# An attention block on one core: smaller weight transfers, a rearranged set-up and loop, and no zero products on TensorE

## What is computed

```python
mod = swish(c) @ w_mod + b_mod            # six rows of 144 per image
xn  = ln(x) * (1 + sc_msa) + sh_msa
q, k, v = heads(xn @ w_qkv + b_qkv)       # 16 heads of 9
q, k = ln(q) * g_q, ln(k) * g_k
o   = softmax(q @ k.T / 3) @ v
x   = x + g_msa * (o @ w_proj + b_proj)
x   = x + g_mlp * (gelu((ln(x) * (1 + sc_mlp) + sh_mlp) @ w1 + b1) @ w2 + b2)
```

## Time and profile before

| | us |
|---|---|
| median of three runs (165.75 to 166.16) | 165.94 |
| the profiled execution | 165.81 |
| its span, first to last instruction | 164.0 |
| outside the span | 1.81 |

### The profile page before, as it was taken

One profiled execution on the slowest core, in us unless ns is written; L12 is line 12 of the kernel. 1 busy time (PEld: TensorE's weight loads), 2 busy tenths in 40 slices (PEclk: granted clock), 3 DMA queues, 4 the chain that ended last, 5 costly groups with the idle time before them and its releaser, 6 DMA issues.

```text
span 164.0 us, 3704 instructions
## 1 busy us (share of the span) xinstructions
PE 142.3 (87%) x1364; PEld 70.7 (43%) x1364; DVE 117.8 (72%) x319; ACT 109.5 (67%) x181; POOL 73.6 (45%) x111
## 2 busy tenths in 40 slices
PE   7558972597978998989989989999999979999991
PEld 2251641232332543523525335336456457574771
DVE  5377688129879496895995979948637999965642
ACT  3143132259799889988898899977998592937300
POOL 4064034516549155087580404586787489000000
PEclk9985555569999999999999999999999999999999
DMA  2329203473723105023050070220000000202022
GB/s 51 111 49 309 77 11 66 102 296 136 152 60 91 41 0 128 4 63 68 2 128 4 0 130 4 64 64 4 0 4 2 0 0 4 72 0 72 4 72 74
DMA packets 22139, 10.33 MB, mean 63 GB/s; under 512 B 17548, under 2 KB 21798, under 8 KB 22120
## 3 DMA queue, kind: packets, MB, share of 16 engines
q1 hardware_dynamic: 21842, 9.77, 23.0%
q10 hardware_dynamic: 278, 0.31, 0.6%
HBM read 4.69 MB, written 1.19 MB: 36 GB/s over the span
## 4 chain that ended last, share of the span: by engine, by line
PE 60%; ACT 12%; DVE 6%; issue 4%; DMA 3%; POOL 2%; DVEq 0%; ACTq 0%; SPq 0%
PE ps_o L1305 15%; PE ps_o L1362 10%; PE ps_s L1285 9%; PE ps_s L1343 6%; ACT pT L647 6%; PE ps_o L1314 5%; PE ps_x L1206 2%; PE ps_x L1212 2%; PE ps_x L1208 2%; PE ps_x L1207 2%; ACT z L596 2%; DMA qT<-qst 2%; PE ps_s L1346 1%; ACT zhi L595 1%; DMA out<-yo 1%
## 5 line engine op out<-in xcount | busy, mean ns | idle before, releaser
L647 ACT ACTIVATE pT<-ps_s 128x1024 f32<-128x1024 f32 x64 | 62.3, 1020 | 9.9 <-PE ps_s L1285 7.3
L1305 PE MATMUL ps_o<-pT,v 128*32 128x256 f32 x512 | 37.6, 388 | 0.4 <-DVE xall L992 0.3
L1285 PE MATMUL ps_s<-qT,kT 32*128 32x256 f16 x256 | 24.9, 279 | 9.6 <-ACT pT L647 4.9
L1285 PEld LDWEIGHTS ps_s<-qT,kT 32*128 32x128 f16 x256 | 7.7, 93 | 32.3 <-ACT pT L647 16.6
L438 POOL TENSOR_TENSOR qg<-qn,gbc 128x288 f32<-128x288 f32 x8 | 7.5, 940 | 24.8 <-DVE qn L851 17.7
L1305 PEld LDWEIGHTS ps_o<-pT,v 128*32 128x32 f32 x512 | 11.9, 108 | 14.4 <-issue 8.8
L406 POOL TENSOR_SCALAR z<-xall,mv,rstd 128x144 f32<-128x144 f32 x14 | 14.2, 1022 | 8.0 <-DVE rstd L1436 8.0
L1362 PE MATMUL ps_o<-w_hi,h_hi 128*128 128x144 f16 (+1 forms) x80 | 16.5, 230 | 0.0
L510 POOL TENSOR_SCALAR z<-xall,mv,rstd 128x144 f32<-128x144 f32 x16 | 14.6, 926 | 3.9 <-DVE rstd L1436 3.9
L835 DVE TENSOR_REDUCE ssum<-sq 128x64 f32<-128x576 f32 x8 | 6.0, 748 | 14.4 <-ACT sq L604 14.3
L1362 PE MATMUL ps_o<-w_lo,h_hi 128*128 128x144 f16 (+1 forms) x80 | 16.2, 225 | 0.0
(11 more groups left out here) (162 smaller groups left out, 294.6 us busy)
## 6 DMA issues: line engine op xcount, KB each, us to landing
gates<-mod_rows SPq DMA_DIRECT2D x8, 216.0 KB, 4.3
out<-yo SPq DMA_DIRECT2D x3, 288.0 KB, 2.3
xall<-in_x SPq DMA_DIRECT2D x1, 576.0 KB, 5.8
xall<-in_x SPq DMA_DIRECT2D x1, 432.0 KB, 4.8
wm<-in_w_mod SPq DMA_DIRECT2D x1, 324.0 KB
out<-yo SPq DMA_DIRECT2D x2, 144.0 KB, 1.8
w_f<-in_w SPq DMA_DIRECT2D x1, 243.0 KB
wq_f<-in_w_qkv ACTq DMA_DIRECT2D x1, 182.2 KB
```

Source lines behind the costliest of these rows:

```text
L647: nc.scalar.activation(pT[(n * U + u) % NP][:].rearrange("p g n -> p (g n)"), ps_s[:, 2 * (u % 2):2 * (u % 2) + 2, :].rearrange("p a n -> ...
L1285: mm = nc.tensor.matmul(ps_s[:, 2 * (u % 2) + a, half * N:(half + 1) * N], kT[n % 2][rows, i, j, :], qT[n % 2][rows, :, j, :], start=True, ...
L1305: mm = nc.tensor.matmul(ps_o[SLOT * g:SLOT * (g + 1), n % 2, jj * N:(jj + 1) * N], v[n % 2][:, at:at + SLOT], pT[(n * U + u) % NP][:, g, : ...
```

## The change

All of it is order, placement and transfers; the arithmetic is the same.

- The zero products, `warm` and the tile `zeros` are gone.
- `w_qkv` and `w1` come in single-block transfers of 36, 20 and 16 rows (`load_main`, `load_third`) and one of a row; the second part of `w_qkv` is issued by SP. `gqk` is issued by POOL. Image 1 comes alone, before the wait for `w_qkv`; images 2 and 3, then 4 to 7 behind it.
- On DVE, image 0's Newton steps and standardising stand before the activation of the condition `c_s`. Image 1 has statistics of its own (`second_stats`); those of images 2 and 3 come after the set-up of image 0. Q's bias (high half) and `id16` are made by ACT, image 0's product with the gains by DVE.
- Image 0's `kst` and `qst` are transposed by PE (16 products with the identity), copied out by DVE (`kT`) and ACT (`qT`); SP's `turn(0)` is gone.
- The second modulation columns and the gate rows go to `ps_o`, so scores of image 0 no longer wait for `mGB`.
- POOL standardises image 1 behind `second_stats` and image 2 behind `next_stats`, clearing the second `v` tile between them.
- The lists of the loop have another order on ACT, DVE and PE. On PE, Q of n+2 comes before values 4 and scores 7; scores 0 of n+1 behind values 6, scores 1 behind values 7, then the projection of n-1.

```diff
-            load_rows(act, wq_f, w_qkv, ld_wq)
+            load_main(act, wq_f, w_qkv, ld_wq)
+        def load_main(eng, tile, w, load):
+            for c in range(NC - 1):
+                eng.dma_start(tile[c * CW:(c + 1) * CW, 0, :], w[0:CW, c, :]).then_inc(load, 16)
+            eng.dma_start(tile[P - TOP:P, 0, :], w[0:TOP, NC - 1, :]).then_inc(load, 16)
...
         @block.sync
-            sp.dma_start(gqk[:, 0, :], g_q.rearrange("(o c) -> o c", o=1)).then_inc(ld_g, 16)
...
+            load_third(sp, wq_f, w_qkv, ld_wq)
             sp.wait_ge(ld_id, 16)
             sp.wait_ge(ld_wa, 32)
-            sp.wait_ge(ld_wq, 16 * 4)
+            sp.dma_start(xall[:, 1, :], x[1].rearrange("(p i) c -> p (i c)", i=I)).then_inc(ld_x1, 16)
+            sp.wait_ge(ld_wq, 16 * 8)
...
-            turn(0)
...
         @block.gpsimd
+            pool.dma_start(gqk[:, 0, :], g_q.rearrange("(o c) -> o c", o=1)).then_inc(ld_g, 16)
...
+            slots_shift(0, prep)
+            pool.wait_ge(second_stats.root.sem, second_stats.root.after(0, "rstd"))
+            standardise(1)
+            slots_shift(1, prep)
+            clear_v(1)
+            ones_v(1)
             pool.wait_ge(next_stats.root.sem, next_stats.root.after(0, "rstd"))
-            standardise(1)
-            slots_shift(0, prep)
-            gains(0, prep)
-            slots_shift(1, prep)
             standardise(2)
...
         @block.scalar, iteration(n)
                 if n:
                     exponentials(n, 0)
+                if n + 1 < B:
+                    v_slots(n + 1)
+                if n:
+                    exponentials(n, 1)
                 if n == 1:
                     x_roots(rest_stats)
-                if n + 1 < B:
-                    roots(n + 1, prep)
...
                 if n + 2 < B:
                     z_high(n + 2, prep)
...
                 if n + 2 < B:
                     squares(n + 2, prep)
...
+                exponentials(n, U - 1)
+                if n + 2 < B:
+                    roots(n + 2, prep)
...
         @block.vector, iteration(n)
-                if n:
-                    heads_out(n - 1)
-                    denominators(n - 1)
                 if n + 1 < B:
                     if n == 1:
                         x_newton(rest_stats)
-                    norm_qk(n + 1, prep, residual, n - 2)
+                    norms(n + 1, prep)
+                if n:
+                    heads_out(n - 1)
+                if n + 1 < B:
+                    scaled_k(n + 1, prep)
...
+                    scaled_q(n + 1, prep)
                     split_k(n + 1, prep)
-                    split_q(n + 1, prep)
+                    split_q_high(n + 1, prep)
...
                 if n + 2 < B:
                     z_low(n + 2, prep)
+                if n + 1 < B:
+                    split_q_low(n + 1, prep)
...
         @block.tensor
-            pe.wait_ge(cleared.sem, cleared.after(0, "zeros"))
-            warm(ps_x[:, 1, :], 6)
             pe.wait_ge(ld_g, 32)
...
-            warm(ps_x[:, 1, :], 8)
...
             transpose_z(1, prep)
+            pe.wait_ge(prep.dve.sem, prep.dve.after(0, "klo"))
+            transpose_heads(kst, 0, first_pe)
+            pe.wait_ge(prep.dve.sem, prep.dve.after(0, "qlo"))
+            transpose_heads(qst, 1, first_pe)
```

More of the change, by code:

```diff
@@ L236, in build @@
         first_stats = Stats(sem, "first_stats", range(I))
-        next_stats = Stats(sem, "next_stats", range(I, 4 * I))
+        second_stats = Stats(sem, "second_stats", range(I, 2 * I))
+        next_stats = Stats(sem, "next_stats", range(2 * I, 4 * I))
         rest_stats = Stats(sem, "rest_stats", range(4 * I, B * I))
@@ L453, in _ @@
             nc.gpsimd.memset(shift[:].bitcast(F32), 0.0).then_inc(pool_set.sem, 1)
[L454 to L457, removed]
+            ones_v(0)
+            pool.wait_ge(ld_wa, 32)
+            thrice(0, SC_A)
+            pool.wait_ge(wm3_made, 2)
             pool.wait_ge(set_dve.sem, set_dve.after(0, "centred3"))
@@ L624, in _ @@
             z_high(0, prep)
+            act.wait_ge(ld_id, 16)
+            nc.scalar.activation(id16[:], id32[:], ACT.Copy).then_inc(id16_made, 1)
+            act.wait_ge(set_pe.sem, set_pe.after(0, "bq"))
+            nc.scalar.activation(wq_3[BROW:KQ, :], ps_s[BROW:KQ, 1, 0:QKV], ACT.Copy, scale=1.0 / ONE).then_inc(bq_high, 1)
             with act.If(needs_max(act) == 1):
@@ L634, in _ @@
             squares(0, prep)
-            x_roots(next_stats)
-            act.wait_ge(pool_set.sem, pool_set.after(0, "o1"))
+            x_roots(second_stats)
             v_slots(0)
@@ L639, in _ @@
             z_high(1, prep)
+            act.wait_ge(first_pe.sem, first_pe.after(0, "qT"))
+            nc.scalar.activation(qT[0][:].rearrange("p t j n -> p (t j n)"), bank16(1).rearrange("p t j n -> p (t j n)"),
+                                 ACT.Copy).then_inc(q_first, 1)
             act.wait_ge(set_dve.sem, set_dve.after(0, "escale"))
@@ L680, in iteration @@
                     z_high2(0)
-                for u in range(4, U):
+                for u in range({0: 5, B - 1: 4}.get(n, 3), U - 1):
                     exponentials(n, u)
@@ L695, in _ @@
             exponentials(0, 0)
+            exponentials(0, 1)
             squares(1, prep)
-            exponentials(0, 1)
+            x_roots(next_stats)
+            roots(1, prep)
             for n in range(B):
@@ L768, in _ @@
             nc.vector.tensor_copy(flag[:], flagf[:]).then_inc(D.sem, 1)
+            x_newton(first_stats)
+            dve.wait_ge(first_stats.root.sem, first_stats.root.after(0, "rstd"))
+            for i in range(I):
+                nc.vector.tensor_scalar(z0[:, i, 0:H], xall[:, 0, i * H:(i + 1) * H], mv[:, i, 0:1], rstd[:, i:i + 1],
+                                        ALU.subtract, ALU.mult).then_inc(first_z.sem, 1)
             dve.wait_ge(set_act.sem, set_act.after(0, "c_e"))
@@ L1156, in columns @@
                                 (CB, wm[0:r, h, shift + P:shift + H]))[j]
-                        mm = nc.tensor.matmul(ps_s[0:m, 0, at:at + B], w, c_s[0:r, h, :], start=(h == 0), stop=(h == 1))
+                        mm = nc.tensor.matmul(mod_bank(k)[0:m, at:at + B], w, c_s[0:r, h, :], start=(h == 0), stop=(h == 1))
                 mm.then_inc(set_pe.sem, 1)
-            def warm(bank, count):
-                for _ in range(count):
-                    nc.tensor.matmul(bank, zeros[:, 0:P], zeros[:], start=True, stop=True)
             def shifted(rows, big, third, w, cols):
@@ L1241, in _ @@
             with pe.If(needs_max(pe) == 1):
-                pe.wait_ge(set_dve.sem, set_dve.after(0, "id16"))
+                pe.wait_ge(id16_made, 1)
                 pe.wait_ge(hot_set, 1)
@@ L1386, in iteration @@
                 scores(n, 6)
-                values(n, 4)
-                scores(n, 7)
                 if n + 2 < B:
@@ L1397, in iteration @@
                         shifted(ps_x[BROW:KQ, f, 0:MLP // 2], sh2, sh23, w1_f, slice(f * MLP // 2, (f + 1) * MLP // 2))
+                values(n, 4)
+                scores(n, 7)
                 values(n, 5)
+                values(n, 6)
                 if n + 1 < B:
                     scores(n + 1, 0)
-                values(n, 6)
-                if n == B - 1:
+                else:
                     transpose_z2(1)
                 values(n, 7)
-            pe.wait_ge(late_dve.sem, late_dve.after(0, "mGB"))
+                if n + 1 < B:
+                    scores(n + 1, 1)
+                    if n:
+                        project(n - 1)
             scores(0, 0)
             scores(0, 1)
-            pe.wait_ge(prep.dve.sem, prep.dve.after(0, "qn"))
+            pe.wait_ge(k_first, 1)
+            pe.wait_ge(q_first, 1)
             make_qkv(1, prep)
```

260 lines of the change are left out of this document (152 added, 108 removed).

## The result

The changed kernel takes 169.0 us (median of four runs, 167.6 to 169.5), the kernel before 166.05 beside it: a ratio of 1.015, 95% interval 1.011 to 1.019. It is slower by 1.5%, where 164.6 was forecast and 167.2 was the upper end of the range. Executions of one kernel lie up to 6 us apart, and each ratio here compares the faster executions alone, so it can be lower than the medians suggest. The profiled execution takes 169.47 us, its span 167.7; that is 3.7 more than before.

A forecast was written before the change was run, and what follows sets the result against it. Set-up bound by a chain of handoffs with no engine full; the loop by PE's list, with 0.6 us of wait per iteration. -1.4 + 2.0 - 1.9 = -1.3 on 165.81: 164.5, as median 164.6; range 162.2 to 167.2.

The forecast's parts named there:

- Iteration 1: Second loop iteration: DVE's Newton steps wait for ACT's roots and PE stands still about 3 us; a loss of 2.0 us.
- E: Start of the first exponential of iteration 1, forecast at 43.3 against 44.73 before, 1.4 us earlier.
- The term of +2.0: Iteration 1's loss: 1.1 for the later Q3 plus 0.9 for values 4 and scores 7 now behind it.
- rival 3: Set-up and iteration 0: without zero products the clock comes back only behind Q2, +2 to +2.5, 166.8 us; chance 0.12.
- Iterations 2 to 5: Loop: image halves one exponential earlier and roots moved on ACT; period 10.43, gain 0.47 each, -1.9 us in four.
- The walk: One iteration of 2 to 5 traced through the engines' lists: PE 10.26 us of its own, period 10.43.
- Rival 4: Loop: q's DMA transposition lands late for scores 0, POOL beside DVE slowing it; period 11.3, 168.1 us; chance 0.12.
- The set-up: Before the loop: image 0's squares at 17.9 (-1.65) and first scores at 27.5, 3.0 us earlier.
- The gains over POOL's queue: Set-up: the `gqk` transfers issued by POOL, for which no row exists, charged a loss of 1.0 us.
- the way from image 0's squares to the first scores: Set-up: squares at 17.9, first scores at 27.5; 1.0 plus 0.35 earlier beyond the 1.65, with PE transposes replacing DMA.
- The zero products: Set-up: the 14 products buy 0.85 us on the 16 modulation columns and nothing after; removal charged +0.85.
- `gains(1)`: Iteration 0: image 1's gains, behind POOL's standardising, copy and clears, forecast at 37.0 against 38.44 before.

The follow-up runs named there:

- e4: The changed kernel with the 14 zero products and their tile put back: 167.3 us, ratio 1.001 to the kernel before.
- f2: The changed kernel with Newton later, third exponential earlier, gains by SP, 128 skipped instructions and zero products back: 157.15 us, ratio 0.942 to the kernel before.
- f3: Changed kernel with Newton later, third exponential earlier, gains by SP, skipped code, zero products, eight set-up fillers, and eight more unread products in iteration 0: 158.85 us.
- e1: The changed kernel with DVE's Newton steps for images 4 to 7 moved behind image 2's scaled q: 164.8 us, ratio 0.989 to the kernel before.

## Why the prediction was wrong

1. **Iteration 1** is the step that failed. Its list work was right: DVE begins at E + 2.69 (forecast 2.85, though its terms add up to 2.80), `kn` at E + 4.58 (4.85). But Q3 and all behind it were priced with durations at 2.4 GHz, though the same paragraph has PE standing still for 3 us. The term of +2.0 measured +5.8 up to the first projection: 2.3 of wait, near the forecast, 4.1 of clock, and 0.6 less than before for the rest of the list. The prediction dealt with the clock in the set-up and in rival 3, which asked only whether it comes back in time, never whether it falls again. The Trainium skill (TensorE: Matmul & The Clock Gate, Part 1) says that the gate follows how busy PE has been of late; the trace agrees, 1.00 ahead of the gap and 0.50 behind it.
2. **Iterations 2 to 5** were to give 1.9 and gave 0.8. The walk was better than its result: without late transpositions the period is 10.2 (10.43 forecast), a gain of 2.7 in four. Rival 4 named the place, q landing too late, and the slack of 0.3 to 0.5 us; its cause, POOL beside DVE, is not it. What ate 1.9 us were two code loads, a resource that neither the prediction nor its rivals had.
3. **The set-up** came out near its sum by errors that cancel, which is luck. The gains over POOL's queue were charged 1.0 and cost 2.17. The Trainium skill (DMA: Bandwidth & Descriptors, Specifications) gives a first byte about 0.4 us later on that queue; here the second transfer landed 3.5 us after its issue, where by SP the product that waits for it started 1.9 after, so the measurement decides. Against that, the way from image 0's squares to the first scores took 8.85 us instead of 9.6, and the clock came back at 27 us, ahead of Q1, not behind it.
4. **The zero products** were charged 0.85 on the columns and nothing after. In the kernel before they are worth nothing that could be seen, in the changed one about 2 (1.7 by the medians of `e4`, 2.2 by those of `f2`), as they keep the clock up for Q0 too, and the path runs through it.
5. **E** at 43.47 (43.3 forecast) hides two more cancelling parts: `gains(1)` came at 35.30 instead of 37.0, and the clock that fell behind the 1.82 us gap took it back, about half of it in Q2 (2.6 us from its first product to the squares, where Q1 took 1.7). Rival 3 was right that Q2 runs at 1.2 GHz, for another reason.

Left open: what places the clock's falls in the set-up and in iteration 0, which lie elsewhere in almost every version; and by what rule a code load starts, since the skipped instructions moved the loads, but not all by the same distance.

## What to carry to other kernels

When a change makes PE wait, price the wait and then ask what the clock does behind it: here 3.4 us of idle time cost 4.1 more afterwards, and two lines moved in another engine's list took both away. Look at the queues of instruction loads in the trace beside every transfer with little slack; where they meet, code that is never executed is a cheap way to move them, and a few added instructions can bring them together (`f3`). A step that had cover before (something slower beside it, as `z` was for the columns) has to be priced anew when the change removes the cover.

## What the runs showed of the hardware

- In eleven of the fourteen traces a 16 KB instruction load ran within the first 2.5 us after the issue of a q transposition and held it up, 23 times in all; these landed 3.5 to 4.6 us after their issue, every other one after 2.7 to 2.9. Every load that was under way in the first 2.2 us did so; of the four that began 2.3 to 2.5 us after the issue, one did (`e1`, 4.45 us).
- The two transfers of the gains (9 numbers each) landed 2.2 and 3.5 us after their issue over POOL's queue; over SP's the product that waits for both started 1.9 us after the second issue.
- The granted clock of a stretch reads 1.00 until the first change that the trace holds, whatever the clock is: in the changed kernel it reads 1.00 from 0 to 27 us, but Q0's products of 432 columns (16 to 18 us) are 0.36 us apart and Q1's, from 28.4 us on, 0.18. Ahead of the first change the durations tell the level.
